# Parts of q and k stored once instead of once per pair, and loaded as three sets of rows

## Time and profile before

| | |
|---|---|
| median of 3 runs | 1015.16 us (1013.94 to 1015.71) |
| profiled execution, its own time | 1016.33 us |
| its span | 1014.5 us |
| mean granted clock of TensorE | 0.993 |
| HBM read, written | 222.03 MB, 51.92 MB |
| first stage | to about 254 us |
| attention | first score 254.4 us, last 779.0 us |
| third stage | from about 779 us |

### The profile page before, as it was taken

How to read it: one execution, slowest core, us unless ns; L and a number is a source line. 1 busy time by engine, 2 the same in 40 slices (tenths; PEclk the granted TensorE clock), 3 DMA queues, 4 the chain that set the end, 5 groups by cost and what they waited for, 6 DMA issues and landing times.

```text
span 1014.5 us, 19566 instructions
## 1 busy us (share of the span) xinstructions
PE 978.4 (96%) x6670; PEld 737.7 (73%) x6736; DVE 836.9 (82%) x1983; ACT 749.5 (74%) x1234; POOL 691.2 (68%) x365
## 2 busy tenths in 40 slices
PE   7999999999899999999999999999998899999998
PEld 6889988999565565655656565656665699999897
DVE  6699999997968999999999999999997555555562
ACT  6754575546689999999999999999998444444444
POOL 2666766764257988989989899988987644444210
PEclk9999999999999999999999999999999899999999
DMA  8748878879999999999999999999998422221001
GB/s 266 262 143 279 268 249 313 306 245 324 375 306 407 383 395 397 380 390 356 393 376 352 375 355 390 378 351 372 340 340 225 133 85 67 74 75 42 22 22 42
DMA packets 141396, 275.26 MB, mean 271 GB/s; under 512 B 19938, under 2 KB 76002, under 8 KB 141170
## 3 DMA queue, kind: packets, MB, share of 16 engines
q1 hardware_dynamic: 140866, 273.93, 76.5%
q10 hardware_dynamic: 432, 0.07, 0.0%
HBM read 222.03 MB, written 51.92 MB: 270 GB/s over the span
## 4 chain that ended last, share of the span: by engine, by line
PE 58%; ACT 25%; DMA 5%; DVE 4%; issue 3%; POOL 3%; SPq 1%; POOLq 0%; DVEq 0%; ACTq 0%
PE psH L615 17%; PE psO L615 16%; ACT t_bt L950 14%; PE psT L731 10%; ACT t_pt L840 6%; PE psV L744 4%; PE psS L720 4%; PE psQ L615 3%; DMA t_ks<-sc_qk 3%; PE psA L615 2%; POOL t_bt L1481 1%; SPq L276 1%; ACT t_mb L972 1%; DMA t_bt<-in_fside_Bx16xSxS 1%; ACT t_cv L840 1%
## 5 line engine op out<-in xcount | busy, mean ns | idle before, releaser
L1481 POOL TENSOR_TENSOR t_bt<-t_bt,t_mb 128x1024 f32<-128x1024 f32 x198 | 418.7, 2149 | 54.3 <-DMA t_bt<-in_fside_Bx16xSxS 54.3
L1280 DVE CUSTOM_DVE_ANT_0 t_bt<-psS,t_bt 128x512 f32<-128x512 f32 x512 | 337.9, 686 | 29.0 <-PE psS L720 26.7
L950 ACT ACTIVATE t_bt<-t_bt,t_nm 128x512 f32<-128x512 f32 x512 | 346.0, 721 | 4.5 <-DVE t_nm L1280 4.5
L731 PE MATMUL psT<-t_idf,t_bt 128*128 128x128 f32 x2048 | 310.8, 275 | 10.7 <-ACT t_bt L950 8.9
L731 PEld LDWEIGHTS psT<-t_idf,t_bt 128*128 128x128 f32 x2048 | 251.0, 141 | 71.7 <-ACT t_bt L950 22.2
L720 PE MATMUL psS<-t_ks,t_qs 128*128 128x512 bf16 x466 | 177.3, 380 | 5.7 <-DMA t_ks<-sc_qk 2.9
L840 ACT ACTIVATE t_pt<-psT 128x512 f32<-128x512 f32 x268 | 159.6, 596 | 24.1 <-PE psT L731 23.5
L1290 DVE COPY t_pt<-psT 128x512 f32<-128x512 f32 x244 | 167.3, 686 | 7.4 <-PE psT L731 7.4
L744 PE MATMUL psV<-t_pt,t_vs 128*17 128x512 f32 x1024 | 135.0, 602 | 0.0
L720 PEld LDWEIGHTS psS<-t_ks,t_qs 128*128 128x128 bf16 x512 | 49.9, 97 | 89.1 <-DVE t_nm L1280 84.1
L877 ACT ACTIVATE psH<-psH,t_bi 128x512 f32<-128x512 f32 x64 | 42.3, 662 | 73.1 <-PE psH L615 70.0
(11 more groups left out here) (176 smaller groups left out, 1936.8 us busy)
## 6 DMA issues: line engine op xcount, KB each, us to landing
t_bt<-in_fside_Bx16xSxS SPq DMA_DIRECT2D x256, 512.0 KB, 7.4
sc_qk<-t_parts SPq DMA_DIRECT2D x64, 384.0 KB, 6.3
t_qs<-sc_qk SPq DMA_DIRECT2D x64, 256.0 KB, 6.2
t_ks<-sc_qk SPq DMA_DIRECT2D x64, 256.0 KB, 7.1
t_wo_f<-in_L_cond_Wo SPq DMA_DIRECT2D x8, 1024.0 KB, 6.1
sc_qk<-t_parts SPq DMA_DIRECT2D x32, 256.0 KB, 8.0
t_wi_f<-in_L_cond_Wi SPq DMA_DIRECT2D x7, 1024.0 KB, 8.8
sc_v<-t_v SPq DMA_DIRECT2D x8, 544.0 KB, 8.0
```

Source lines behind the costliest of these rows:

```text
L731: ins = e.transpose(psT[turned_bank(n)][:, kk, :], bt[u % NB][:, t, kk * 128:(kk + 1) * 128], idf[:, :])
L950: e.activation(p, p, ACT.Exp, bias=nm[:, n % NR:n % NR + 1], scale=-1.0).then_inc(a_exp, 1)
L1280: e.tensor_tensor_reduce(bt[u % NB][:, t, :], s, bt[u % NB][:, t, :], -1.0, 3.0e38, ALU.add, ALU.min, nm[:, n % NR:n % NR + 1]).then_inc(v ...
L1481: e.tensor_tensor(bt[u % NB][:, hs, :], bt[u % NB][:, hs, :], mb[b % 2][:, hs, :], ALU.add).then_inc(g_M, 1)
```

## The change

- `TERMS` lists the same 8 pairs in another order: the k parts run 0 1 2 0 1 2 0 1 as before, the q parts 1 2 0 2 0 1 0 1.
- The scratch has 4 places: k's parts 0, 1, 2 once each, and q's parts in the order 1, 2, 0, 1. A store writes a part once (q's part 1 twice), for parts 1 and 2 both halves in one DMA: 5 DMAs for q and 4 for k per sequence.
- A load takes four heads at a time, as three DMAs for q and three for k: to rows 0 to 47 (slots 0 to 2), 48 to 95 (slots 3 to 5) and 96 to 127 (slots 6, 7). q's sets begin at places 0, 1 and 2, k's all at place 0. A row is 4 KB. There are 12 DMAs per group instead of 8, at n % 32 = 4 and 16 (`QK_STEP` = 12), and for g = 1 at n = 20 and 21.
- The late stores are 8 instead of 12, again every 12 tiles from n = 28. Waits count the new numbers of DMAs.

```diff
-PT = 16 * 6
+PT = [16 * 5, 16 * 4]
-TERMS = [(0, 0), (0, 1), (0, 2), (1, 0), (1, 1), (1, 2), (2, 0), (2, 1)]
+TERMS = [(1, 0), (2, 1), (0, 2), (2, 0), (0, 1), (1, 2), (0, 0), (1, 1)]
-QK_STEP, ROWS_AT = 6, (184, 248, 312, 376, 440)
+QK_STEP, ROWS_AT = 12, (184, 248, 312, 376, 440)
-        sc_qk = dram("sc_qk", [B, 2, NK, NP3, 128, S], BF16)
+        sc_qk = dram("sc_qk", [B, 2, NK, 4, 128, S], BF16)
-        late_stores = range(28, 28 + 12 * 12, 12)
+        late_stores = range(28, 28 + 8 * 12, 12)
...
                 if a == 0:
                     P.wait_ge(a_p0, 4 * b + 2 * n + mt + 1)
+                    load(d_p[b % 2][n], sc_qk[b, n, mt, 0 if n else 2], parts[b % 2][n][:, 0, mt, :])
                 elif a == 1:
                     P.wait_ge(a_p1, 2 * b + n + 1)
+                    for place in (1,) if n else (0, 3):
+                        load(d_p[b % 2][n], sc_qk[b, n, :, place].rearrange("m p s -> p m s"), parts[b % 2][n][:, 1, :, :])
                 else:
                     P.wait_ge(g_p2, 2 * b + n + 1)
-                g = slice(a, NP3, 3) if n else slice(3 * a, min(3 * a + 3, NP3))
-                k = len(range(NP3)[g])
-                load(d_p[b % 2][n], sc_qk[b, n, mt, g].rearrange("i p s -> p i s"), parts[b % 2][n][:, a:a + 1, mt, :].broadcast_to([128, k, S]))
+                    load(d_p[b % 2][n], sc_qk[b, n, :, 2 if n else 1].rearrange("m p s -> p m s"), parts[b % 2][n][:, 2, :, :])
...
-                hs = slice(2 * i, 2 * i + 2)
+                hs = slice(4 * i, 4 * i + 4)
...
-                for dst, w in ((qs, 0), (ks, 1)):
-                    load(d_q[n % 2], dst[n % 2][:, hs, :], sc_qk[b, w, half].rearrange("i (d h) s -> (i d) h s", d=HD)[:, hs, :])
+                for dst, w, first in ((qs, 0, (0, 1, 2)), (ks, 1, (0, 0, 0))):
+                    rows_ = sc_qk[b, w, half].rearrange("a (d h) s -> (a d) h s", d=HD)
+                    for j in range(3):
+                        to = slice(3 * j * HD, min(3 * j + 3, NP3) * HD)
+                        load(d_q[n % 2], dst[n % 2][to, hs, :], rows_[first[j] * HD:first[j] * HD + to.stop - to.start, hs, :])
...
-                if n < N and 0 <= m < 4 * step and m % step == 0 and n // 32 + 1 < 2 * B:
+                if n < N and 0 <= m < 2 * step and m % step == 0 and n // 32 + 1 < 2 * B:
...
-                P.wait_ge(d_q[g % 2], 128 * (g // 2 + 1))
+                P.wait_ge(d_q[g % 2], 192 * (g // 2 + 1))
```

More of the change, by code:

```diff
@@ L335, in store_part @@
                     P.wait_ge(a_p0, 4 * b + 2 * n + mt + 1)
+                    load(d_p[b % 2][n], sc_qk[b, n, mt, 0 if n else 2], parts[b % 2][n][:, 0, mt, :])
                 elif a == 1:
                     P.wait_ge(a_p1, 2 * b + n + 1)
+                    for place in (1,) if n else (0, 3):
+                        load(d_p[b % 2][n], sc_qk[b, n, :, place].rearrange("m p s -> p m s"), parts[b % 2][n][:, 1, :, :])
                 else:
                     P.wait_ge(g_p2, 2 * b + n + 1)
-                g = slice(a, NP3, 3) if n else slice(3 * a, min(3 * a + 3, NP3))
-                k = len(range(NP3)[g])
-                load(d_p[b % 2][n], sc_qk[b, n, mt, g].rearrange("i p s -> p i s"), parts[b % 2][n][:, a:a + 1, mt, :].broadcast_to([128, k, S]))
+                    load(d_p[b % 2][n], sc_qk[b, n, :, 2 if n else 1].rearrange("m p s -> p m s"), parts[b % 2][n][:, 2, :, :])
             def store_parts(b, a):
-                for i in range(4):
-                    store_part(b, i // 2, a, i % 2)
+                for n in range(2):
+                    for mt in range(1 if a else NK):
+                        store_part(b, n, a, mt)
             def store_v(b):
@@ L405, in load_qk @@
                     for w in range(2):
-                        P.wait_ge(d_p[b % 2][w], PT * (b // 2 + 1))
-                for dst, w in ((qs, 0), (ks, 1)):
-                    load(d_q[n % 2], dst[n % 2][:, hs, :], sc_qk[b, w, half].rearrange("i (d h) s -> (i d) h s", d=HD)[:, hs, :])
+                        P.wait_ge(d_p[b % 2][w], PT[w] * (b // 2 + 1))
+                for dst, w, first in ((qs, 0, (0, 1, 2)), (ks, 1, (0, 0, 0))):
[3 more added lines that the diff above has]
+                        load(d_q[n % 2], dst[n % 2][to, hs, :], rows_[first[j] * HD:first[j] * HD + to.stop - to.start, hs, :])
             def load_mask(b):
@@ L428, in first_attention_loads @@
                 load_mask(0)
-                for i in range(4):
+                for i in range(2):
                     load_qk(0, i)
@@ L461, in attention_loads @@
                     i = late_stores.index(n)
-                    store_part(B - 1, 1 - i // 6, i % 6 // 2, i % 2)
+                    store_part(B - 1, 1 - i // 4, max(i % 4 - 1, 0), i % 4)
                 if n == 88:
@@ L465, in attention_loads @@
                     for w in range(2):
-                        P.wait_ge(d_p[0][w], PT * B // 2)
+                        P.wait_ge(d_p[0][w], PT[w] * B // 2)
                     P.wait_ge(d_v, 16 * B)
@@ L471, in attention_loads @@
                 if n == 104:
-                    P.wait_ge(d_p[1][1], PT * B // 2)
+                    P.wait_ge(d_p[1][1], PT[1] * B // 2)
                 if n == ROWS_AT[0]:
-                    P.wait_ge(d_p[1][0], PT * B // 2)
+                    P.wait_ge(d_p[1][0], PT[0] * B // 2)
                 if n in load_w_at:
@@ L896, in qkv @@
                         P.wait_ge(v_bq, 1)
-                        P.wait_ge(d_p[b % 2][n], PT * (b // 2))
+                        P.wait_ge(d_p[b % 2][n], PT[n] * (b // 2))
                         e.activation(parts[b % 2][n][:, 0, mt, :], qk_bank(b, n, mt)[:, :], ACT.Identity, bias=bqk[:, n, mt:mt + 1]).then_inc(a_p0, 1)
```

## The result

The changed kernel takes **1098.59 us** (median of 4 runs, 1096.38 to 1101.21), the kernel before 1015.25 us in the same comparison: a ratio of **1.083, interval 1.081 to 1.086**, 83 us slower. The prediction had the direction and the mechanism, but 1027 us in a range to 1055. The profiled execution has a span of 1098.3 us.

What follows compares the result with a forecast made beforehand. Attention was taken as bound by its engines, TensorE, VectorE and ScalarE, with DMA having 8% to spare. Terms -1.7 + 11.6 + 1.5 = +11.4 us took the median from 1015.2 to 1026.6, forecast 1027 us, range 1012 to 1055.

Steps and rivals of the forecast that it cites:

- Direction and mechanism: In attention: slower, as DMA becomes the bound by a little; 1017.2 to 1045 us, chance 0.47.
- The landmark on ScalarE: A 1.32 us entry in the chain of waits, every 64 tiles, 62.74 us apart before; 64.3 us expected.
- The stores at 0: Smaller q and k stores, in the first stage and at attention's beginning, were to change the time by 0.
- the writes less by 18.9 MB: HBM writes over the whole kernel were to fall by 18.9 MB in any case.
- The early end of the loads at -1.7: Each group's last q/k load goes out at n % 32 = 16 instead of 22, removing late loads' cost: -1.7 us.
- no wait of TensorE for q and k after the second group: Sign of being right, in attention: TensorE no longer waits for q and k loads after group two.
- The first loads at +1.5: First loads of the second q/k buffers, twelve issues in one block, land later: +1.5 us, bounds -1.3 and +3.6.
- The loads' shape: Attention's q/k loads reaching only some partitions move slower: +1.7 us a step, 3.4 us a group of 8 heads.
- the factor 2.06 on all bytes: Upper bound for the q/k loads: all bytes take 2.06 times as long, +2.75 us a step, 5.5 a group.
- What the margin absorbs: In attention DMA has 2.6 us spare per group (2.5 in four early ones), leaving +11.6 us over fourteen groups.
- stalls in bursts: Sign of being wrong: VectorE stalls right after each load step while the mean DMA rate stays under its limit.
- All rows pay: Rival: the middle set of q/k loads is no better than the others, 5.5 us a group; 1058 us, chance 0.18.

Runs made afterwards that it cites:

- e_sets_only: Kernel before with only each two-head load of q and k split into rows 0-47, 48-95 and 96-127; old stores: 1106.87 us, ratio 1.093.
- e_sets_four: The change's loads (three sets of rows, four heads) with the old stores and 8 scratch places, against the kernel before: 1098.51 us, ratio 1.085.
- e_stores_two: Kernel before with the change's stores and full-height two-head loads, q and k each from its own places: 1016.33 us, ratio 1.002.
- e_four_heads: Kernel before with full-height loads of four heads at n % 32 = 4 and 16: 1010.29 us, ratio 0.997.
- e_double: Kernel before with full-height four-head loads, both steps of groups 2 to 15 loaded twice: 1064.21 us, ratio 1.050.
- f_single: Kernel before with full-height four-head loads, only the first step of groups 2 to 15 loaded twice: 1028.50 us, ratio 1.016.
- e_spread: The change with one set of q and of k every three tiles instead of six DMAs at a time: 1163.42 us, ratio 1.148.
- e_stores_only: Kernel before with the change's stores and full-height two-head loads, q and k both read from q's places: 1037.93 us, ratio 1.028.
- p_source: Loads-only kernel, bias loads mixed with q/k load shapes: full height 55.4 us, three sets 65.1, both loads from the same bytes 55.0.
- p_shapes: Loads-only kernel, each DMA shape by itself, 3 MiB per phase: full height 10.7 us, the three sets in turn 16.1.

## Why the prediction missed, point by point

- **Direction and mechanism: right.** DMA share near 1 with fewer GB/s, bias landings above 7.4 us, POOL's waits for bias up by 82 us and VectorE's 66.8 us for POOL are as written. The chain has more in it than was foretold: bias loads are 13% of the span, and loads of k 11% (3% before). The landmark on ScalarE, expected 64.3 us apart, comes 75 to 77 us apart. The place is right: e_sets_only and e_sets_four bear the whole loss, the stores none.
- **The stores at 0, the writes less by 18.9 MB: right** (e_stores_two, at most 3 us of loss; 18.87 MB).
- **The early end of the loads at -1.7: right as a term** (e_four_heads, -2.9 us, interval -1.3 to -4.6). In the change it buys nothing, since k is late anyway: TensorE waits 23.0 us for it in 13 places, where "no wait of TensorE for q and k after the second group" was foretold. That line was wrong. The load went out 15.7 us ahead, and in the chain it takes as long as that:

```profile
363.61 15.86 DMA t_ks<-sc_qk
...
516.93 16.28 DMA t_ks<-sc_qk
```

- **The first loads at +1.5: right.** The chain shows the last of them at 301.15 us, 8.23 us to its landing, 1.2 us later than before.

```profile
301.15 8.23 DMA t_ks<-sc_qk
```

- **"The loads' shape": here it failed.** The step said "+1.7 us a step, 3.4 us a group". The runs show 7.6 us a group, 3.8 per MiB (6.8 and 3.4 in e_sets_four). It went wrong where it costed the sets by themselves: their own slowness was right in sum (1.8 per MiB alone), but among full-height loads in one queue they cost more than that, 2.1 to 4.0 per MiB in the open mixes of loads and 3.4 to 6.3 in the kernel. Its upper bound, "the factor 2.06 on all bytes", was built from the same assumption. The range took its end from there, and so ended 44 us too low. No row of before showed loads of this kind in company: the earlier trace rows show four small loads with nothing else in the queue, and the earlier trace rows, stores amid a full queue, gave 1.8 and so pointed to less, not to more. The estimate that the prediction worked out from the map of ports in the Trainium skill, "SBUF — State Buffer", "Door 1: The DMA port swizzle", +2.6 us per MiB and 1054 us, fits neither measurement: it is above the 1.8 of sets alone and below the 3.8 in the kernel.
- **"What the margin absorbs": too large.** 2.6 us were read off a window at 405 GB/s of 32 us length. e_double and f_single put the level that lasts at 384 to 398, the margin at 1.0 to 1.5. The row of 308 to 435 us, at 392 GB/s with engines not quite full, was the better reading of the limit. This is the smaller error: with a margin of 1.5 and the forecast's 3.4 a group, 14 x 1.9 = 27 us instead of 11.6.
- **The sum with the measured terms.** (7.6 - 1.5) x 14 = 85 us, and 1.2 for the first loads; measured 83. This is bookkeeping and no test, since the 7.6 was read off the period of the same kernel: it says that 14 groups of 37.5 instead of 31.45 us are the whole loss.
- **The alternative it named, stalls in bursts: fell** with e_spread. "All rows pay", the nearest rival, was wrong in its mechanism too: the middle set does move faster than the others (13.0 us for 3 MiB), and the total is larger still.

**What stays open.** The open mixes without a kernel account for 2.1 to 2.4 of the 3.8 us per MiB, and for 4.0 of 6.3 apart. The rest appears only in the kernel. Idle DMA engines explain little of it: there are single microseconds with a share down to 0.69 (615 to 616 us), but over twelve groups the share is 1.00, beside 1.02 in e_double and 1.03 in e_spread. That is some 1 us of the 7.6 a group as an estimate, and nothing of e_spread's price. So the engines are occupied and move less, and why by so much more than in the probes isn't known. Why two loads of the same bytes cost e_stores_only 24 us, and nothing in p_source, is open as well.

## What to carry to other kernels

A transfer that reaches only part of the partitions must be priced with its neighbours: in a queue near its limit ask when the full-height loads beside it will land, and when its own last piece will, not only how long it takes alone. If a load has to be split, split it so that each piece spans all partitions (even and odd rows, every fourth row). Where several loads raise one semaphore, look at the landing of the last one. Read a margin off the longest window in which the DMA engines were truly the bound, or press them once with doubled loads; a short window flatters it.

## What the hardware showed that had not been expected

- Sets of rows within a part of the partitions cost more among full-height loads than alone: with k alone in sets and q at full height a mix loses 7.5 us, with both in sets 8.6; with the same sets each between two bias loads 16.1, where p_shapes gives 8.9 for them.
- In the changed kernel the last set of a step lands in 12.8 us (7.1 before), and the bias loads in 13.5 (7.4 before).
- Two pieces of 64 rows: 1008 us as even and odd rows, 1119 us as halves.
